# Perceiver layer on one core: head 0's keys and maxima moved into the projection, loops written out, and three smaller moves

## What is computed

```python
x = x + cross_attention(layernorm(x), ctx)   # 16 heads of 32: q = xn@Wq+bq, k = ctx@Wk+bk, v = ctx@Wv+bv
                                             # softmax(q k^T / sqrt(32)) over 8192 keys, then relu(o@W1+b1)@W2+b2
x = x + local_attention(layernorm(x))        # rotary, a causal window of 256, then @Wout
x = x + ffn(layernorm(x))                    # w_gate, w_up, w_down and inputs rounded to FP4 in blocks of 16
```

## Time and profile before

| | |
|---|---|
| median of 3 runs | 1485.82 us (1484.34 to 1488.38) |
| profiled execution, its own time | 1484.56 us |
| its span | 1482.8 us |
| PE busy | 1356.4 us, 91% |
| DVE busy | 1123.3 us, 76% |
| ACT busy | 808.7 us, 55% |
| POOL busy | 799.0 us, 54% |
| mean granted TensorE clock | 0.955 |

### The profile page before, as it was taken

The page is one execution under the profiler, slowest core; times in us unless marked ns, Lnnn a source line. Parts: engine busy times, 40 slices in busy tenths (PEclk is TensorE's granted clock), DMA queues, the critical chain, the costliest instruction groups (busy, mean ns, idle before and its releaser), DMA issues. The chain is left out here.

```text
span 1482.8 us, 43758 instructions
## 1 busy us (share of the span) xinstructions
PE 1356.4 (91%) x16736; PEld 651.1 (44%) x16736; DVE 1123.3 (76%) x1834; ACT 808.7 (55%) x1529; POOL 799.0 (54%) x307
## 2 busy tenths in 40 slices
PE   6999999968999999999999999999999897885898
PEld 3444444421344444444444444444444443453444
DVE  7477777768888887887887878878886654676797
ACT  3454444430566776666766766767667722474211
POOL 2122222232599898997997988979987001100111
PEclk9999999985899999999999999999999998898899
DMA  6578787765033222122212212221210030770000
GB/s 232 166 199 224 211 227 215 226 170 148 22 125 89 71 69 67 36 70 69 70 36 71 68 40 60 68 67 36 70 57 27 4 135 0 165 155 1 0 8 22
DMA packets 129452, 140.76 MB, mean 95 GB/s; under 512 B 44848, under 2 KB 110256, under 8 KB 127216
## 3 DMA queue, kind: packets, MB, share of 16 engines
q1 hardware_dynamic: 129264, 138.08, 32.8%
HBM read 77.23 MB, written 44.17 MB: 82 GB/s over the span
## 5 line engine op out<-in xcount | busy, mean ns | idle before, releaser
L1168 DVE TENSOR_REDUCE attend_part_max<-attend_banks 128x1 f32<-128x512 f32 x1024 | 635.9, 683 | 132.0 <-PE attend_banks L903 130.3
L1131 ACT ACTIVATE attend_prob<-attend_banks 128x512 f32<-128x512 f32 x1024 | 531.4, 603 | 234.9 <-PE attend_banks L955 229.6
L1316 POOL TENSOR_TENSOR early<-early,attend_prob 128x1024 f32<-128x1024 f32 x210 | 618.8, 2947 | 34.8 <-ACT attend_prob L1131 5.9
L903 PE MATMUL attend_banks<-attend_k_stack,attend_q_pre 96*32 96x512 f16 x4096 | 423.4, 401 | 31.1 <-DMA attend_k_stack<-k_scratch 16.4
L955 PE MATMUL attend_banks<-attend_q_now,attend_k_stack 97*32 97x512 f16 x4096 | 362.2, 386 | 14.3 <-ACT attend_prob L1131 14.3
L966 PE MATMUL attend_banks<-attend_prob,attend_vh 128*32 128x512 f32 x2048 | 265.2, 594 | 0.0
L955 PEld LDWEIGHTS attend_banks<-attend_q_now,attend_k_stack 97*32 97x32 f16 x4096 | 112.2, 97 | 164.1 <-ACT attend_prob L1131 104.5
L903 PEld LDWEIGHTS attend_banks<-attend_k_stack,attend_q_pre 96*32 96x32 f16 x4096 | 112.4, 96 | 126.6 <-DVE attend_part_max L1168 39.2
L977 PEld LDWEIGHTS attend_banks<-attend_prob,ones 128*32 128x32 f32 x3048 | 87.5, 109 | 159.5 <-issue 159.5
L977 PE MATMUL attend_banks<-attend_prob,ones 128*32 128x128 f32 x3048 | 126.9, 272 | 0.0
L413 POOL TENSOR_TENSOR project_w_whole<-project_grid,project_qscale 128x704 f32<-128x704 f32 x24 | 35.5, 1481 | 128.7 <-DVE project_grid L538 128.7
(11 more groups left out here) (160 smaller groups left out, 1423.5 us busy)
## 6 DMA issues: line engine op xcount, KB each, us to landing
v_scratch<-project_v SPq DMA_DIRECT2D x16, 1024.0 KB, 5.7
attend_k_stack<-k_scratch SPq DMA_DIRECT2D x64, 256.0 KB, 3.5
attend_vh<-v_scratch SPq DMA_DIRECT2D x16, 1024.0 KB, 5.2
early<-in_ctx_dram SPq DMA_DIRECT2D x16, 768.0 KB, 7.4
k_scratch<-project_k_hi SPq DMA_DIRECT2D x64, 128.0 KB, 2.7
k_scratch<-project_k_lo SPq DMA_DIRECT2D x64, 128.0 KB, 2.9
attend_k_stack<-k_scratch SPq DMA_DIRECT2D x64, 128.0 KB, 3.5
late<-in_L_xattn_W_dram SPq DMA_DIRECT2D x2, 2048.0 KB, 10.7
```

Of the source, the lines that this page charges most:

```text
L903: last = nc.tensor.matmul(pre_ps[c * HD:(c + 1) * HD, bank, :], q_pre[0:KROWS, s, queries], k_stack[0:KROWS, s, part * BLK:(part + 1) * BL ...
L1131: nc.scalar.activation(prob[:, q % PSLOTS, t, :], s_ps[:, s_bank[BT * q + t]], ACT.Exp, scale=SCALE).then_inc(p_ready, 1)
L1168: nc.vector.tensor_reduce(part_max[:, s, j, part:part + 1], pre_ps[:, bank], AX.X, ALU.max).then_inc(pre_read, 1)
L1316: nc.gpsimd.tensor_tensor(sums, sums, prob[:, q % PSLOTS, 0:n], ALU.add).then_inc(pool_summed, 1)
```

## The change

1. **Head 0's keys and maxima in the projection.** The keys of head 0 (32 rows of group 0 of each block) are also stored straight into a stack in SBUF (`k_first`), with three more transfers to a block on SP. In blocks 2 to 15 PE puts the 64 tiles of head 0 between the groups and tiles of the projection, at eight numbered places of a block (place 0 to 3 behind key group 0 to 3, 4 to 7 behind value tile 0 to 3). Here a tile is one matmul. There is one PSUM bank for them (`pre_ps`), and a tile waits until all tiles before it are read; only for the last eight there are four banks. DVE reads them (`maxima`) at the places shown below. The row of head 0 is made at the end of the projection. The attention block begins with 8 tiles of head 1 in place of 72.
2. **Loops written out** on all engines, in the projection and in attention.
3. **Barrier without store waits.** SP's waits for the key, value and weight stores go from the end of the projection to where the data is used.
4. **Denominators between scores.** `"den"` in `PE_ORDER`.
5. **First loads reordered.** `x` is loaded behind the second block of context rows. The layer norm of `x` moves behind the keys of block 0, and POOL's addition of `b2` behind the first three units.

The per-head copies of the queries (`q_pre`, `q_now`) and their transfers go: PE reads `q_stack` in place.

```diff
-PE_ORDER = ((0,), 0, (1,), 1, 2, (2,), 3, (3,))
+PE_ORDER = ((0,), 0, (1,), 1, "den", 2, (2,), 3, (3,))
...
+            pre_ps = ps("pre_ps", [P, BLK])
...
+            PLACES = 2 * G
+            tiles_at = {(b, at): [] for b in range(NB) for at in range(PLACES)}
+            for j in range(TT):
+                tiles_at[2, 2 * j + 1].append((0, j))
+                tiles_at[3, 2 * j].append((1, j))
+                tiles_at[3, 2 * j + 1].append((2, j))
+                for b in range(4, NB - 1):
+                    tiles_at[b, 2 * j + 1].append((b - 1, j))
+                tiles_at[NB - 1, j].append((NB - 2, j))
+                tiles_at[NB - 1, min(G + j + 1, PLACES - 1)].append((NB - 1, j))
...
+            def pre_bank(n):
+                turn = n - (len(tile_order) - LAST_BLOCK_TILES)
+                return pre_ps[:] if turn < 0 or turn % 4 == 0 else yT_ps[:, turn % 4 - 1]
+            def reads_before(n):
+                turn = n - (len(tile_order) - LAST_BLOCK_TILES)
+                return n if turn <= 0 else n - 3 if turn >= 4 else 0
```

SP, behind the eight key stores of a block, and its waits at the end:

```diff
+                    for at, half in enumerate((k_hi, k_lo, k_hi)):
+                        sp.dma_start(k_first[at * HD:(at + 1) * HD, (2 * i + u) * BLK:(2 * i + u + 1) * BLK],
+                                     half[0:HD, u, 0]).then_inc(k_out[u], 16)
...
-                for u in range(2):
-                    sp.wait_ge(k_out[u], NB // 2 * 2 * HG * 16)
-                    sp.wait_ge(v_out[u], NB // 2 * 16)
-                for w in range(3):
-                    sp.wait_ge(w_unit_out[w], NB // 2 * 16)
```

DVE:

```diff
+                def maxima(b, at):
+                    for part, j in tiles_at[b, at]:
+                        n = tile_order.index((part, j))
+                        dve.wait_ge(pre_ready, n + 1)
+                        nc.vector.tensor_reduce(part_max[:, 0, j, part:part + 1], pre_bank(n), AX.X,
+                                                ALU.max).then_inc(pre_read, 1)
...
                         for g in range(G):
                             key_low(i, u, g)
                             quantize(AFTER_KEYS[g])
+                            if g:
+                                maxima(2 * i + u, g - 1)
+                        if i == 0 and u == 0:
+                            dve.wait_ge(x_in, 16)
+                            layer_norm_vector(dve, chain, var_ready, sd_ready, 1, xn_q, xn_ready)
                         if not (last and u == 1):
                             y_low(i, u)
-                        quantize(AFTER_Y[u])
+                        maxima(2 * i + u, G - 1)
+                        quantize(AFTER_Y[u] - 3)
+                        for t in range(BT):
+                            maxima(2 * i + u, G + t)
+                            quantize(1 if t < 3 else 0)
```

PE, called behind each key group with g and behind each value tile with G + t:

```diff
+                def maxima(b, at):
+                    for part, j in tiles_at[b, at]:
+                        n = tile_order.index((part, j))
+                        if n == 0:
+                            pe.wait_ge(q_stacked, 16 * 3 * HG)
+                        if j == 0:
+                            pe.wait_ge(k_out[part % 2], 16 * K_OUTS * (part // 2 + 1))
+                        if n == len(tile_order) - LAST_BLOCK_TILES:
+                            pe.wait_ge(ylo_ready, NB)
+                        wait(pe, pre_read, reads_before(n))
+                        nc.tensor.matmul(pre_bank(n), q_stack[0:KROWS, 0, j * P:(j + 1) * P],
+                                         k_first[0:KROWS, part * BLK:(part + 1) * BLK], start=True,
+                                         stop=True).then_inc(pre_ready, 1)
```

Attention:

```diff
-            FIRST_TILES = TT * (QUADS + AHEAD)
+            FIRST_TILES = TT * AHEAD
...
                         for step in PE_ORDER:
-                            if isinstance(step, int):
+                            if step == "den":
+                                if q >= 2:
+                                    add_to_denominator(i, s, q - 2)
+                                elif not first:
+                                    add_to_denominator(*before, QUADS - 2 + q)
+                            elif isinstance(step, int):
                                 scores(i, s, q, step)
...
-                with pe.Fori(1, LASTPAIR) as i:
+                for i in range(1, LASTPAIR):
```

More of the change, by code:

```diff
@@ L416, in unit @@
                                             ALU.mult).then_inc(wq_ready, 1)
+                for w in range(3):
+                    unit(0, w)
+                pool.wait_ge(wq_ready, 3)
                 pool.wait_ge(b2_in, 16)
@@ L422, in _ @@
                 pool.wait_ge(x_biased, 1)
-                for w in range(3):
-                    unit(0, w)
-                with pool.Fori(1, NB // 2) as i:
+                for i in range(1, NB // 2):
                     for w in range(3):
@@ L483, in _ @@
                     nc.scalar.activation(q_hi[:, g], k_ps[:, g % 2], ACT.Identity, bias=bq[:, g:g + 1]).then_inc(qhi_ready, 1)
-                with act.Fori(1, NB // 2 - 1) as i:
-                    two_blocks(i, False)
-                two_blocks(NB // 2 - 1, True)
+                for i in range(1, NB // 2):
+                    two_blocks(i, i == NB // 2 - 1)
+                act.wait_ge(row_ready, 1)
+                nc.scalar.activation(q_stack[KROWS:KROWS + 1, 0, :], pre_ps[KROWS:KROWS + 1, :], ACT.Copy).then_inc(row_set, 1)
             @block.vector
@@ L581, in _ @@
                     nc.vector.tensor_tensor(q_lo[:, g], qf[:, g], q_hi[:, g], ALU.subtract).then_inc(qlo_ready, 1)
[L582 to L584 removed]
+                for i in range(1, NB // 2):
+                    two_blocks(i, i == NB // 2 - 1)
+                dve.wait_ge(pre_read, TT * QUADS)
+                nc.vector.tensor_reduce(neg_max[:, 0], part_max[:, 0], AX.X, ALU.max, negate=True).then_inc(max_ready, 1)
             @block.tensor
@@ L664, in _ @@
                 pe.wait_ge(qhi_ready, G)
-                with pe.Fori(1, NB // 2 - 1) as i:
+                for i in range(1, NB // 2 - 1):
                     two_blocks(i)
@@ L672, in _ @@
                 values(i, 1)
+                pe.wait_ge(max_ready, 1)
+                for t in range(TT):
+                    last = nc.tensor.matmul(pre_ps[KROWS:KROWS + 1, t * P:(t + 1) * P], neg_max[:, 0, t:t + 1], identh[:],
+                                            start=True, stop=True)
+                last.then_inc(row_ready, 1)
         piece = carve(late)
@@ L889, in _ @@
                 store_o(LASTPAIR + 1, 0)
+                for w in range(3):
+                    sp.wait_ge(w_unit_out[w], NB // 2 * 16)
                 sp.wait_ge(o_in[DK - 1], 16 * (1 + 2 * TT))
@@ L1321, in _ @@
                         add_up(0, s, q)
-                with pool.Fori(1, LASTPAIR) as i:
+                for i in range(1, LASTPAIR):
                     for s in range(2):
```

190 lines of the change are left out of this document (95 added, 95 removed).

## The result

The changed kernel takes 1532.13 us (median, 1528.88 to 1533.0) against 1487.1 for the kernel before, measured beside it (1484.34 to 1489.54): a ratio of 1.031, 95% interval 1.0287 to 1.0332. It is slower, as forecast (1525, between 1484 and 1550). Its profiled execution took 1528.88 us at a span of 1526.9, with a mean granted clock of 0.949.

What follows compares the result with a forecast made beforehand. PE was taken to bound the projection, with DVE's order of steps close behind in u = 0 blocks. 106.6 us come and 65.5 go: 1484.56 + 41 = about 1525 us, range 1484 to 1550.

Steps and rivals of the forecast that it cites:

- (e): Projection, blocks 4 to 13: tiles in one bank wait for DVE's reads; a pair takes 48.7 against 36.2, +62 us.
- The rival that one bank is enough: Projection: DVE reads the tile of place 1 before PE ends group 3; 1439 us, chance 0.11.
- The clock in (e): Blocks 4 to 13: slower clock behind PE's stops, 1.7 us for each u = 0 block, 0.5 for each u = 1.
- (f): Block 2: PE waits 6.5 us for the stacked queries, 1.6 more at place 3; with tiles and clock +9.7.
- (g): Block 3, tiles at all eight places: PE waits for `key_low`, rounding steps and reads; +19 us (14 to 22).
- (h): Block 14 of the projection goes from 18.7 to 27.5 us: +8.8 (5 to 12).
- (a): Start of attention, maxima alone: 8 of 72 tiles stay, 7.7 us in place of 51.9; 44.2 saved.
- (i): Block 15 and barrier: late tiles, about 7 us wait for own keys, 3 saved on stores; +7.1 (4 to 11).
- (c): First loads: block 0's rows come some 2 us earlier, the moved layer norm gives most back; 0.5 us saved.
- (b): Attention: the five turns of the loop go, 20.8 us saved; nothing taken for the projection's loops.
- written-out code is no faster: Rival, attention: the turns' loss comes back in straight code, 20.8 us is not saved; 1546 us, chance 0.06.
- (d): Attention, denominators in mid-quad: the work is the same, taken as 0, with 7 us saved and 6 lost as ends.

## Why the prediction came out right, and where it was off

**The read behind the late step (e): right, in mechanism and size.** 49.1 a pair for 48.7. The stops stand where they were put, at place 3, 6.9 to 7.5 us and 3.2 us, on the chain that was worked out. Removing the load from it shortens the one kind, moving the reads ahead of the rounding steps removes the other (block 5 of that run), both together leave at most 0.6 us of it, and taking the tiles out takes it all. The rival that one bank is enough was wrong for this order but right for another: with tiles and reads moved, the same one bank costs little. That the time is then 1440.92, where the rival said 1439, is luck: the first exponential comes 13.1 us earlier than in the kernel before, for the rival's 24.7, and attention gains 30.7 for 20.8.

**The clock in (e): right in size.** 2.2 a pair was taken, 1.7 and 0.5. Where the clock came back when PE was kept busy, a block with u = 0 was 1.6 or 2.2 shorter and one with u = 1 1.5, which is 0.6 on the mean of the five; that only 1.4 a pair came back is because it did not come back everywhere. All six stops of 6.9 to 7.5 us (blocks 4 to 14, u = 0) have the 12 transposes at 2.77 behind them, at half clock. Behind the five stops of 3.19 (u = 1) they take 1.48 three times, 1.67 and 2.07. The rule of the Trainium skill (TensorE: Matmul & The Clock Gate, HAM oscillation), by which matmuls between waits start at half rate, was borne out by every long stop and by two of the five short ones.

**(f), (g), (h), (a)** each came within 3 us.

**(i), 9.0 for 7.1.** The wait for block 15's own keys is there, 7.6 us, as worked out.

**(c), +2.8 for -0.5, the end of its range passed.** The step that failed: the term has nothing for the clock. The first keys come 2.6 to 2.8 earlier and the stop behind the layer norm takes 2.3 to 3.2, which nearly cancel, as was said. But in the changed kernel's profile the clock is at 0.54 from 16 to 20 us, and at 0.67 for 4 us behind the stop. In the run with the denominators back, whose projection is the same, it is at full speed throughout, in spite of a stop of 3.2, and block 1 ends at 52.2 (before: 52.0), not at 54.8. The changed kernel, then that run:

```profile
32.00:36.00 4.00, 3.86 (x12) 0.67 0.31 70
```

```profile
12.00:40.00 28.00, 23.20 (x107) 1.00 0.68 220
```

The three more transfers and the fill on GpSimd, the rival of the run on the first loads, are in both. Of the eight kernels with this stop, six show a slow clock behind it and two do not; why is open.

**(b), the step that failed.** The prediction had it that "heads written out take 48.9 like those within a turn", from rows 11, which show no head that is written out. They take 50.07. The turns gave the 20.8, but writing ACT out takes about 12.7 back (1092.1 - 1079.4, all written out against ACT's loop kept), so loops alone gave 7.9 in attention. The rival "written-out code is no faster" was nearer to the truth of this edit than its chance of 0.06 says.

**(d), the step that failed.** Since the work is the same, it was taken at 0. It puts work ahead of scores 2 and 3, so that PE no longer stands still at the fourth score of a quad, and gave 24.4 in the changed kernel (1093.5 - 1069.1). Much of that is the other side of (b): it makes good the lag of ACT, which only written-out code has. Heads of 48.9 with ACT's loop against 48.7 with `"den"`, and 4.1 behind the last row, leave some 7 us to it by itself, as an estimate, the end of the range that was given; no run has `"den"` with ACT's loop kept.

**Not tested.** No run has the barrier without store waits by itself; its 3 us stand in (i) as an estimate only.

**The sum.** Attention gained 30.9 for 20.8, and the first exponential came 75.0 later for 62, the 13 spread over (a), (c) and (e) to (i). These misses have opposite signs, and so have those of (b), 13 us, and (d), 24 us, within attention. That the span's +44.1 lies 3 us from the forecast is in part luck.

## What to carry to other kernels

Before work is put between the steps of a pipeline, write down for each piece where its consumer stands in that engine's order, and what that engine waits for ahead of it: the tiles of ten blocks cost 64.5 us where their reads stood behind a late load and rounding steps, and 14.3 in the same one bank where the reads, and some of the tiles, stood elsewhere. A queue's order counts too: one transfer issued a block earlier gave another 20 us. A written-out part of the old kernel is the sample of what written-out code costs; read its rows before you price a loop.

## What was not expected of the hardware

- ScalarE's exponential starts 0.52 us or more (mostly 0.52 or 0.53) behind the start of its matmuls in written-out code and 0.44 or 0.45 in its loop (700 to 800 us of each kernel, exponentials that waited for over 0.9 us). In this kernel that made a loop on ScalarE faster than none, while TensorE's loop cost 3 to 8 us a turn.
- TensorE's turn costs more when all other engines are written out: 55.7 to 57.9 for the head across it, less 50.1, against 53.4 less 48.9 before. Which of the other engines matters was not tried.
- At the start VectorE's copy of the identity took 6.88 us, beside a fill of one partition on GpSimd; without that fill 0.23. First the changed kernel, then the one with the first loads moved:

```profile
2.57 6.88 DVE L546 CAST identh<-ident 128x128 f16<-128x128 f32 x1 [2.57 <-DMA ident<-in_c_ident_dram]
...
0.73 8.63 POOL L448 MEMSET k_first<- 1x10240 f16 x1 [0.29 <-POOLq L2017]
```

```profile
2.59 0.23 DVE L494 CAST identh<-ident 128x128 f16<-128x128 f32 x1 [2.59 <-DMA ident<-in_c_ident_dram]
```

The copy ends with the fill. PE's first keys come at 13.79 and 13.64, so nothing was lost by it here. The Trainium skill (Trainium Architecture — The Big Picture, What this means for kernel authors) says that of all engines only VectorE and GpSimd contend for SBUF, by a port pair that one of them locks; these rows agree, but the two were not tried by themselves.
